# Search scores of two heads in the two row halves of TensorE's array

## The reference

```python
q = _lin(xn, Wq, bq).reshape(b, n, H, HD) / np.sqrt(HD)        # H = 16, HD = 8
k = _lin(xn, Wk, bk).reshape(b, n, H, HD)
score = jax.nn.softmax(jnp.einsum('bihd,bjhd->bhij', q, k), axis=-1)
v = _lin(xn, Wv, bv).reshape(b, n, R, HD)
out = jnp.einsum('bhij,bjrd->bihrd', score, v)
...
x = _layernorm(x + search(x))
x = _layernorm(x + local(x))
```

## Time and profile before

| | |
|---|---|
| median of 3 runs | 1532.94 us (1531.63 to 1533.76) |
| the profiled execution | 1539.12 us |
| its span, first to last instruction | 1537.3 us |
| mean granted clock of TensorE | 0.962 of 2.4 GHz |
| PE busy | 1351.8 us, 17408 matmuls |
| DVE, POOL, ACT busy | 973.2, 901.0, 833.8 us |
| packets of DMA | 104457, 57.52 MB |

### The profile page before, as it was taken

One profiled execution on the slowest core, in us unless ns is written; L12 is line 12 of the kernel. 1 busy time (PEld: TensorE's weight loads), 2 busy tenths in 40 slices (PEclk: granted clock), 3 DMA queues, 4 the chain that ended last, 5 costly groups with the idle time before them and its releaser, 6 DMA issues.

```text
span 1537.3 us, 42305 instructions
## 1 busy us (share of the span) xinstructions
PE 1351.8 (88%) x17408; PEld 956.3 (62%) x17408; DVE 973.2 (63%) x1489; ACT 833.8 (54%) x1106; POOL 901.0 (59%) x884
## 2 busy tenths in 40 slices
PE   2899999899998999979998989979999899975775
PEld 1366666666676666756766666756677567753654
DVE  3666666857656766567658576576756676544462
ACT  1265566565665556646665656646566456732442
POOL 3022775667565755567566676646855675766473
PEclk7699999999999999989999999989999999988998
DMA  5410120112110121102111020101211001000101
GB/s 133 138 51 26 45 60 20 37 30 60 31 34 19 30 57 33 33 17 57 28 34 36 19 66 19 38 24 37 56 28 38 9 15 30 19 12 11 25 16 23
DMA packets 104457, 57.52 MB, mean 37 GB/s; under 512 B 81651, under 2 KB 98333, under 8 KB 104221
## 3 DMA queue, kind: packets, MB, share of 16 engines
q1 hardware_dynamic: 100128, 48.52, 12.5%
q10 hardware_dynamic: 4143, 6.31, 1.6%
HBM read 27.28 MB, written 8.39 MB: 23 GB/s over the span
## 4 chain that ended last, share of the span: by engine, by line
PE 61%; POOL 12%; DVE 10%; ACT 6%; issue 5%; DMA 4%; SPq 1%; ACTq 1%; POOLq 0%; DVEq 0%
PE pair L525 53%; PE pair L528 9%; POOL rn L1029 2%; POOL work L1029 2%; DMA h<-yb 2%; DVE work L830 2%; ACT probs L715 2%; DVE gm L914 2%; POOL raw L1029 2%; DVE ss L959 1%; POOL gate L1040 1%; ACT work L715 1%; POOL rstdl L1029 1%; DVE wexp L830 1%; POOL yb L1029 1%
## 5 line engine op out<-in xcount | busy, mean ns | idle before, releaser
L914 DVE TENSOR_REDUCE gm<-pair 128x2 f32<-128x1024 f32 x256 | 304.7, 1216 | 99.5 <-PE pair L525 99.4
L525 PEld LDWEIGHTS pair<-vt,probs 128*64 128x64 f32 x8192 | 273.4, 137 | 59.3 <-ACT probs L715 30.8
L525 PE MATMUL pair<-vt,probs 128*64 128x73 f32 x8192 | 291.5, 229 | 14.7 <-ACT probs L715 9.7
L715 ACT ACTIVATE probs<-pair 128x1024 f32<-128x1024 f32 x256 | 253.4, 1023 | 64.9 <-PE pair L525 61.2
L830 DVE TENSOR_TENSOR work<-pair,rot 128x1024 f32<-128x1024 f32 x128 | 154.7, 1221 | 87.4 <-ACT work L715 85.3
L1029 POOL TENSOR_TENSOR rn<-rn,neg_half 128x16 f32<-128x16 f32 x64 | 187.9, 2936 | 5.3
L525 PE MATMUL pair<-wqkv,h_t 128*128 128x512 f32 x384 | 185.2, 610 | 0.8 <-ACT h_t L715 0.6
L525 PE MATMUL pair<-k_stack,q_stack 96*128 96x512 bf16 x512 | 156.8, 403 | 20.2 <-DVE gm L914 10.7
L525 PE MATMUL pair<-q_stack,k_stack 98*128 98x512 bf16 x512 | 148.3, 384 | 9.2 <-DMA q_stack<-gt 2.6
L1029 POOL TENSOR_TENSOR work<-work 128x1024 f32<-128x1024 f32 x64 | 151.0, 2359 | 0.0
L715 ACT ACTIVATE raw<-pair 128x292 f32<-128x292 f32 x128 | 52.8, 413 | 175.3 <-PE pair L525 174.9
(11 more groups left out here) (129 smaller groups left out, 2506.7 us busy)
## 6 DMA issues: line engine op xcount, KB each, us to landing
v_mix<-v_nat SPq DMA_DIRECT2D x112, 128.0 KB, 2.8
k_stack<-parts_scratch SPq DMA_DIRECT2D x96, 96.0 KB
q_stack<-parts_scratch SPq DMA_DIRECT2D x96, 96.0 KB
parts_scratch<-shared SPq DMA_DIRECT2D x48, 128.0 KB, 2.4
x_in<-in_x SPq DMA_DIRECT2D x8, 256.0 KB, 2.8
h<-yb SPq DMA_DIRECT2D x64, 32.0 KB
out<-yb SPq DMA_DIRECT2D x16, 128.0 KB, 1.8
h<-yb SPq DMA_DIRECT2D x64, 31.8 KB
```

The source lines that it names most:

```text
L525: return pe.matmul(b_out, lhsT, rhs, start=start, stop=stop, skip_group_check=True)
L715: return act.activation(dst, src, fn, **kw)
L914: m = dve.tensor_reduce(gm[:, g % 2, 2 * jj:2 * jj + 2, h % 4], bank("max", b, h, jj), AX, ALU.max, negate=True)
```

## The change

A score now has six of the nine products (the three smallest are left out): 6 x 8 = 48 rows (`ROWS`), 50 with the maximum. Two heads stand one above the other, one from row 0 and one from row 64 of the stacks. Such a pair is a "slot" (`SLOTS` = 8 a batch); `heads_of` and `slot_of` map between slots and heads, h and h + 4. A block of `max` or `st` is now one slot and one tile of 128 queries or keys: two matmuls, one for each head, each into a bank of its own of the pair. There are as many blocks and matmuls of 512 columns as before. `probs` is buffered for two slots, and `pv` of either head of a slot waits for all four blocks of the slot.

The parts now lie in DRAM in six places in stack order; a part that is used in several products is written to each of its places by one DMA with a repeated source (`PLACES`). So the spill still has three DMAs for each of q and k, and writes twice the bytes; the stack reads 48 rows for two heads in each of two DMAs instead of 24 rows for four heads in each of three. For contiguous rows the projection's columns are permuted (`d h` in place of `h d`), which `weigh` does on DVE from a temporary tile, with a permuted load of two bias columns. PE's wait for the search loads moves from `max` to `gturn`. In the plan a block of `max` or `st` is priced at 250 ns in place of 440, and a stack at 900 in place of 1050 and 2100. The rest of the diff, left out here, follows from the new indices.

```diff
@@ -36,6 +36,23 @@
 HID = 341
 HCH = [(0, 114), (114, 114), (228, HID - 228)]
 MASKED = -3.0e38
+PLACES = [[(0, 3, 1), (3, 2, 2), (4, 1, 1)], [(2, 3, 1), (0, 2, 5), (1, 1, 1)]]
+ROWS = 6 * HD
+SLOTS = H // 2
+def slot_of(h):
+    return 4 * (h // 8) + h % 4, h // 4 % 2
+def heads_of(s):
+    return [8 * (s // 4) + s % 4 + 4 * r for r in range(2)]
...
+        here = [(s, j) for s in (2 * g, 2 * g + 1) for j in range(T)]
+        for s, j in here:
+            step(0.75 * (4 * s + j) / 32)
+            add(("max", b, s, j), "PE", 250, [("stack", b, 0, g), ("stack", b, 1, g), quad_before("gsplit", g, 2),
+                                             block_before("rowmax", s, j, 2)], "two", ("rowmax", b, s, j))
+            add(("rowmax", b, s, j), "DVE", 1220, [("max", b, s, j)])
+        add(("gsplit", b, g), "POOL", 500, [("rowmax", b, *sj) for sj in here] + [quad_before("gturn", g, 2)])
         add(("gturn", b, g), "PE", 230, [("gsplit", b, g), quad_before("gstack", g, 1)], "one", ("gcopy", b, g))
         add(("gcopy", b, g), "ACT", 570, [("gturn", b, g)])
         add(("gstack", b, g), "SP", 1300, [("gcopy", b, g)], land=2300)
     for g in range(QUADS):
-        for h in range(4 * g, 4 * g + 4):
-            for jj in range(2):
-                step(0.25 + 0.75 * (2 * h + jj) / 32)
-                add(("st", b, h, jj), "PE", 440, [("gstack", b, g), head_before("pv", h, NHEAD),
-                                               block_before("probs", h, jj, 2)], "two",
-                    ("probs", b, h, jj))
-                add(("probs", b, h, jj), "ACT", 1020, [("st", b, h, jj)], table="exp")
-            add(("pv", b, h), "PE", 2090, [("probs", b, h, 0), ("probs", b, h, 1), ("v_tok", b),
-                                           n("attsum", b - 1, h // 8, T - 1)], "one", ("raw", b, h))
-            add(("raw", b, h), "ACT", 410, [("pv", b, h)])
+        for s in (2 * g, 2 * g + 1):
+            for j in range(T):
+                step(0.25 + 0.75 * (4 * s + j) / 32)
+                add(("st", b, s, j), "PE", 250, [("gstack", b, g), *slot_before(s, 2), block_before("probs", s, j, 2)],
+                    "two", ("probs", b, s, j))
+                add(("probs", b, s, j), "ACT", 1020, [("st", b, s, j)], table="exp")
+            for h in heads_of(s):
+                add(("pv", b, h), "PE", 2090, [("probs", b, s, j) for j in range(T)]
+                    + [("v_tok", b), n("attsum", b - 1, h // 8, T - 1)], "one", ("raw", b, h))
+                add(("raw", b, h), "ACT", 410, [("pv", b, h)])
...
@@ -355,7 +372,7 @@
-STEPS = {"weigh": 3, "fold": 14, "ln1_stats": 2, "ln1_rstd": 2, "gsplit": 2, "logit": 2, "lsum": 2, "weight": 2, "ln2_stats": 2, "ln2_rstd": 2,
...
-
-
-NHEAD = 2
+    return {"spill": 3, "stack": 2, "gstack": 2}.get(kind, 1)
...
@@ -420,7 +440,7 @@
             i, *more = bank_of[name]
             return pairs[i // 2] if more else pairs[i // 2][:, i % 2, :]
-        scratch = nc.dram_tensor("parts_scratch", [2, SPLIT, HD, H, S], BF16, kind="Internal").ap()
+        scratch = nc.dram_tensor("parts_scratch", [2, ROWS // HD, HD, H, S], BF16, kind="Internal").ap()
         ident = sb("ident", [P, P]); identb = sb("identb", [P, P], BF16)
@@ -455,12 +475,13 @@
         parts = shared[:, :].bitcast(BF16).rearrange("p (a c s) -> p a c s", a=2, c=SPLIT)
         hid_s = shared[:, 0:2 * S].rearrange("p (c s) -> p c s", c=2)
         rest = sb("rest", [P, S])
-        qs, ks = sb("q_stack", [P, H, S], BF16), sb("k_stack", [P, H, S], BF16)
-        gm = sb("gm", [P, 2, T, 4])
-        gb = sb("gb", [P, 2, T, 2, 4], BF16)
+        qs, ks = sb("q_stack", [P, SLOTS, S], BF16), sb("k_stack", [P, SLOTS, S], BF16)
+        gm = sb("gm", [P, 2, T, 2, 2])
+        gb = sb("gb", [P, 2, T, 2, 2, 2], BF16)
         gt = sb("gt", [8, S], BF16)
         vt = sb("vt", [P, 2, T, VT])
-        probs = sb("probs", [P, NHEAD, T, S])
+        probs = sb("probs", [P, 2, T, 2, S])
         raw = sb("raw", [P, H, T, RAWC])
         rden = sb("rden", [P, 2, 8, T]); logit = sb("logit", [P, 8, T, R]); lmax = sb("lmax", [P, 2, 8, T])
         lexp = sb("lexp", [P, 8, T, R]); lsum = sb("lsum", [P, 2, 8, T]); lrec = sb("lrec", [P, 2, 8, T])
@@ -498,11 +519,14 @@
         tab = flat[:, 2048:3072].rearrange("p (c t d) -> p c t d", c=4, t=T)
         bv_rd = flat[:, 3072:3072 + RV]
         stack = lambda x: x.rearrange("p h n -> p (h n)")
-        first_loads = [(ident[:, :], t["ident"]), (cols[:, :], t["cols"]), (w_all[:, 0:2 * D], t["w_all"][:, 0:2 * D])]
+        wqk_tmp = flat[:, 3072 + RV:3072 + RV + 2 * D]
+        first_loads = [(ident[:, :], t["ident"]), (cols[:, 2:], t["cols"][:, 2:]), (wqk_tmp, t["w_all"][:, 0:2 * D]),
+                       (cols[:, 0:2], t["cols"][:, 0:2].rearrange("(h d) c -> d h c", d=HD))]
         search_loads = [
             (rows[:, :], t["rows"].partition_broadcast(P)), (identb[:, :], t["identb"]),
-            (stack(ks[NPROD:GUARD + 2, :, :]), t["under"]),
-            (stack(qs[NPROD:GUARD, :, :]), t["under"][0:GUARD - NPROD]),
+            *[(stack(ks[64 * r + ROWS:64 * r + ROWS + 2, :, :]), t["under"][GUARD - NPROD:, 0:SLOTS * S])
+              for r in range(2)],
             (w_all[:, 2 * D:], t["w_all"][:, 2 * D:]), (wqv_tmp, t["WqvT"]),
             (bv_rd, t["bv"].partition_broadcast(P)), (bqv_tmp, t["bqv"].partition_broadcast(P)),
             (tab, t["tables"]), (flat[:, 1536:2048], t["scales"].partition_broadcast(P)),
@@ -549,35 +573,36 @@
                         pe.wait_ge(*upto("weigh", 0))
                         m = mm(z, wqk[a], xf[:, :])
                     elif kind == "max":
-                        h, jj = ix
-                        pe.wait_ge(s_search, 16 * len(search_loads))
-                        pe.wait_ge(*upto("stack", b, 0, h // 4))
-                        pe.wait_ge(*upto("stack", b, 1, h // 4))
-                        for u in range(2):
-                            j = 2 * jj + u
-                            m = mm(z[:, u, :], qs[0:GUARD, h, j * P:(j + 1) * P], ks[0:GUARD, h, :])
+                        s, j = ix
+                        pe.wait_ge(*upto("stack", b, 0, s // 2))
+                        pe.wait_ge(*upto("stack", b, 1, s // 2))
+                        for r in range(2):
+                            rr = slice(64 * r, 64 * r + ROWS)
+                            m = mm(z[:, r, :], qs[rr, s, j * P:(j + 1) * P], ks[rr, s, :])
                     elif kind == "gturn":
                         g, = ix
+                        pe.wait_ge(s_search, 16 * len(search_loads))
                         pe.wait_ge(*upto("gsplit", b, g))
                         for j in range(T):
-                            m = mm(z[0:8, j * P:(j + 1) * P], gb[:, g % 2, j, :, :].rearrange("p c i -> p (c i)"),
+                            m = mm(z[0:8, j * P:(j + 1) * P], gb[:, g % 2, j, :, :, :].rearrange("p r c i -> p (r c i)"),
                                    identb[:, :])
                     elif kind == "st":
-                        h, jj = ix
-                        pe.wait_ge(*upto("gstack", b, h // 4))
-                        for u in range(2):
-                            j = 2 * jj + u
-                            m = mm(z[:, u, :], ks[0:GUARD + 2, h, j * P:(j + 1) * P], qs[0:GUARD + 2, h, :])
+                        s, j = ix
+                        pe.wait_ge(*upto("gstack", b, s // 2))
+                        for r in range(2):
+                            rr = slice(64 * r, 64 * r + ROWS + 2)
+                            m = mm(z[:, r, :], ks[rr, s, j * P:(j + 1) * P], qs[rr, s, :])
                     elif kind == "pv":
                         h, = ix
-                        pe.wait_ge(*upto("probs", b, h, 1))
+                        s, r = slot_of(h)
+                        pe.wait_ge(*latest([("probs", b, s, j) for j in range(T)]))
                         pe.wait_ge(*upto("v_tok", b))
                         for k in range(T):
                             for j in range(T):
                                 for w in range(2):
                                     q0 = k * P + 64 * w
                                     m = mm(z[64 * w:64 * w + 64, k * RAWC:(k + 1) * RAWC],
-                                           probs[:, h % NHEAD, j, q0:q0 + 64], vt[:, b % 2, j, 0:RAWC], j == 0, j == T - 1)
+                                           probs[:, s % 2, j, r, q0:q0 + 64], vt[:, b % 2, j, 0:RAWC], j == 0, j == T - 1)
                     elif kind == "att_turn":
                         for hf in range(2):
                             pe.wait_ge(*upto("attsum", b, hf, T - 1))
@@ -746,11 +771,12 @@
                             for dst, src in layer_loads:
                                 act.dma_start(dst, src).then_inc(s_layers, 16)
                     elif kind == "probs":
-                        h, jj = ix
-                        act.wait_ge(*upto("st", b, h, jj))
-                        if h >= NHEAD or b:
```

(58 more changed lines are left out.)

29 lines of the change are left out of this document (12 added, 17 removed).

## The result

The changed kernel takes 1554.3 us (median of 4 runs, 1553.1 to 1556.1) against 1532.5, a ratio of 1.014 (1.0125 to 1.016). The forecast was 1476, so it is wrong in its sign. The page of the changed kernel, parts 1 and 2: busy time, slices of PE, its granted clock.

A forecast was written before the change was run, and what follows sets the result against it. PE's queue was taken to bound most of the span. PE loses 110 and gains 25 us; 59 in full windows less 2 at the start gives 57, so 1533 - 57 = 1476 us; 8-in-10 range 1437 to 1512.

The forecast's parts named there:

- Side by side: In max and st blocks: two matmuls in opposite row halves run together, 0.216 us instead of 0.43, 110 us off PE.
- The mask row: In s: four mask matmuls on array quarters end 0.41 us after the first starts; in series 0.86.
- The rule of the Trainium skill: In score blocks: loads overlap matmuls in flight only in a different row group; every block showing one would cost 51 us.
- Borders: Between score blocks and whole-array work: 0.09 us at each of 277 sides, 25 us, 15 of them in full windows.
- What reaches the span: Over the whole kernel: of PE's net 85 us, the part in full windows, 74 - 15 = 59 us, shortens the span.
- full window: A 10 us window from 60 us on with PE busy 9.0 us or more; 93 such hold 67% of score matmuls.
- Groups and buffers: In the search: pv waits for four probs blocks, but the other slot's blocks hide its later start; cost nothing.
- a bound of 16 us: In the first search: without that cover each of eight slots waits 2 x 1.02 us more for ACT.
- a lower clock: Sign of being wrong, in PE's slices: a granted clock below 1 in more slices than before; no size given.
- Rival 4: In the plan: new prices give a poor order, 1533 us, or 1574 with all seven periods long; chance 0.08.
- Poor periods of the 190 kind: Between batches' local layers: periods of 190.6 us instead of 171.0; three more than now would cost 59 us.
- Start: At batch 0: the doubled spill of both projections costs +2 us; other start work is hidden.

The follow-up runs named there:

- heads kernels: Runs with both row halves but no slots: a block is one head and two tiles, stacks hold all 16 heads in both halves; 1518.2, 1504.3 and 1466.3 us.
- slots_late_pv: The changed kernel with only the second pv of a slot ranked later, so st blocks stand between the two pv; 1514.8 us.
- heads_new_prices: The changed kernel without slots: a block is one head and two tiles in both row halves, plan prices 250 and 900; 1504.3 us.
- old_order_one_half: heads_old_order, but both matmuls of a block use the lower row half, so they run in series; 1562.2 us.
- heads_old_order: heads_new_prices with the plan prices of the kernel before, so every engine works through exactly the order of before; 1518.2 us.
- heads_ranks: heads_new_prices with three rank constants changed (0.75 to 0.85, 0.25 to 0.35, 1.1 to 1.3), letting the search run later against local layers; 1466.3 us.
- late_pv_ranks: slots_late_pv with the three rank constants of heads_ranks (0.85, 0.35, 1.3); 1506.6 us.
- after_ranks: The changed kernel with the three rank constants of heads_ranks (0.85, 0.35, 1.3); 1554.2 us.

## Why the prediction was wrong

The runs split the way from before to after into four steps: the new shape with its borders +29 us (1533 to 1562), side by side -44 (to 1518), new prices -14 (to 1504), slots +50 (to 1554). Each step has some 5 us of uncertainty. The slot step also takes a load away, since the heads kernels fill both halves with all heads, so grouping itself may cost more than 50.

*Side by side.* Right in size: 0.216 us a block, loads hidden, 114 us of busy PE against 110. The mask row was the right witness. Two blocks in a row end after 0.61 us, 0.22 + 0.39, and the weight loads of the second (85.91 to 86.01) stand inside the first block's matmuls (85.90 to 86.29), in the same halves. The rule of the Trainium skill that I weighed ("TensorE: Matmul & The Clock Gate", Part 3, The mechanism) doesn't hold here: it would have shown 0.32 a block.

*Borders.* Right at 0.09 each. That only 15 of the 25 us would count was probably too low: the whole new shape cost 29, 20 of the 25 between the traces in the six middle periods. How much of that is the borders alone isn't shown.

*What reaches the span.* The step that failed first: the overlap. I took a microsecond off PE in a full window as one off the span: 74 us. Concurrency gave 44 under the old order, and 110 us put back on the changed kernel's PE cost 30. A window at 9 of 10 us doesn't say that its slack stays the same once PE gives way; 66 us of it came back as idle time. In the search alone the trace shows the loop that lay just beneath, 3.74 us under 4.01; for the local layers I have no such loop. Relief brings 40% under the very same order under which the new shape costs at least what its borders add up to. One reading is that they stand elsewhere, the borders beside the local layers, whose steps are on the chain, and the relief in blocks that wait for ACT and DVE next. That is argued and not shown.

*Groups and buffers.* The step that turned the sign. I named the cover (the other slot's blocks hide the later `pv`) and a bound of 16 us for its loss in the first search; slots cost 50 us, and 88 under the other order. The blocks of the other slot couldn't cover, since both `pv` come free together, at 4.2 us in one piece, while only two blocks are allowed in flight, 2.04 us of ACT. ACT's row with its 3.96 us wait shows it, and slots_late_pv, which parts the two `pv`, takes back 40 of the 50 us. The bound was also counted for one search instead of eight.

*Clock.* heads_new_prices and the changed kernel have the same matmuls. Their windows, 60 to 150 us, first the changed kernel (columns as in the earlier trace rows), then heads_new_prices:

```profile
60.00:150.00 90.00, 76.64 (x1373) 56.95 (x1375) 52.81 (x57) 48.26 (x68) 16.79 (x28) 0.86 0.15 47
```

```profile
60.00:150.00 90.00, 78.42 (x1566) 57.32 (x1566) 60.47 (x70) 56.96 (x80) 24.23 (x38) 0.97 0.27 74
```

The busy time is nearly equal, but the changed kernel gets 1373 matmuls done and the other 1566, at 0.86 and 0.97 of the clock. PE's idle time is also nearly equal, 13.4 and 11.6 us; what differs is how it lies. Ahead of the fall at 89.3 PE had worked 2.3 of the 3.4 us from 85.9 on, in short blocks with waits between; the heads kernel has one wait of 0.52 us and then a whole `pv`.

Over the whole span the traces give this, in us. The third column is PE's busy time laid over the clock's records. The last takes half of it off the busy time, an estimate of what the same work is at full clock.

| profiled run | PE busy | of it at 1.2 GHz | PE idle | busy, less half of that |
|---|---|---|---|---|
| before | 1352 | 77 | 185 | 1314 |
| old_order_one_half | 1399 | 95 | 164 | 1351 |
| heads_old_order | 1285 | 100 | 230 | 1235 |
| heads_new_prices | 1281 | 96 | 221 | 1233 |
| after | 1322 | 167 | 230 | 1239 |
| slots_late_pv | 1295 | 107 | 215 | 1242 |
| heads_ranks | 1268 | 58 | 197 | 1239 |
| late_pv_ranks | 1293 | 116 | 203 | 1235 |
| after_ranks | 1324 | 188 | 234 | 1230 |

All kernels with blocks side by side do the same work, 1230 to 1242 us at full clock. Of the 50 us that slots add to the span (heads_new_prices to after) 41 are busy time, some 36 of them by this estimate the lower clock, and only 10 are idle time. My sum had no term for the clock, though a lower clock stood among the signs of being wrong. That the span would be shorter by as much at full clock isn't shown: from execution to execution of one kernel the mean clock moves and the time doesn't follow (old_order_one_half 0.960 at 1564.6 us, 0.947 at 1561.5).

*Order.* Rival 4 had 0.08. The new order was in fact 14 us worse for the old blocks and 14 better for the new, and three constants are worth 14 us to the kernel before, 38 to the heads kernel, 8 to slots_late_pv and nothing to the changed kernel. Poor periods of the 190 kind didn't multiply: the changed kernel's middle periods are even, 156 to 183. What I priced as rival 4 wasn't what happened, but orders alone move the heads kernel by 52 us (heads_old_order to heads_ranks, the same instructions), nearly the whole forecast gain, and the range should have said so.

*Start.* I had +2 us for the doubled spill. The first `max` block of before, then of the changed kernel:

```profile
37.90 1.87 PE L525 MATMUL pair<-k_stack,q_stack 96*128 96x512 bf16 x4 [5.43 <-issue]
```

```profile
32.44 0.61 PE L549 MATMUL pair<-k_stack,q_stack 48*128 48x512 bf16 x2 [13.30 <-DMA q_stack<-parts_scratch]
```

It starts 5.5 us earlier. The spills of k are issued from 21.34 on in 1.57 us rather than 1.91, and their landing releases the stack at 25.03, 3.7 us after the first issue, as before. The time is won behind them: the q stack is issued from 29.63 on (30.13 before), and PE's first block follows 2.8 us later, where it was 7.8. Twice the bytes cost nothing that can be seen in the spills. By the first matmul on `x_b`, at 178 us against 173, the gain was lost again.

## What to carry to other kernels

Before an engine's relief is counted into the span, follow the loop one level down: what the relieved engine waits for next, with how many buffers in flight, over one whole cycle of the loop; here a loop of 3.74 us lay under a PE queue of 4.01. When work is regrouped, count what comes free at one moment and how long it runs in one piece against what is in flight for the engine behind it: two `pv` of 2.1 us against two blocks of 1.02. In a kernel with a planned order, change the prices and the ranks as experiments of their own, since the order can be worth as much as the edit. And compare busy time for the same work: where it grew, as here by 41 us, the clock is a term of its own.

## What the runs showed of the hardware

Matmuls of 48 or 50 rows in the two halves, 128 columns wide and 512 long, into two banks, run side by side at 0.22 us a pair, with their weight loads hidden. A border between this shape and the whole array costs 0.09 us in either direction; 277 of them are 25 us of PE's queue, and the kernel became 29 us slower with all else that the shape brought. The unexpected part is the clock: with the same matmuls and nearly the same idle time (13.4 and 11.6 of 90 us), waits gathered between short score blocks went with a granted clock of 0.86, where single waits between whole `pv` had 0.97, in one trace of each.
